# A rotary sum parted between two engines in a fused attention and feed-forward kernel, with all queues laid anew

## The reference, cut to what matters

```python
h = shift_token(x)
q, k, v = jnp.split(h @ wqkv, 3, axis=-1)          # 8 heads of 64
q = l2norm(q) * qs
k = l2norm(k) * ksc
q = q * cos * scale + rotate_half(q) * sin * scale
k = k * cos / scale + rotate_half(k) * sin / scale
o = local_attention(q, k, v)                        # windows of 64
```

## Time and profile before

| what | value |
|---|---|
| time, median of 3 runs | 1863.35 us (1860.35 to 1864.81) |
| the profiled execution's own time | 1865.29 us |
| its span in the trace | 1863.5 us |
| TensorE matmuls busy | 1598.5 us, 86% |
| VectorE busy | 1239.7 us, 67% |
| ScalarE busy | 926.7 us, 50% |
| GpSimd busy | 594.0 us, 32% |

### The profile page before, as it was taken

One profiled execution on the slowest core, in us unless ns is written; L12 is line 12 of the kernel. 1 busy time (PEld: TensorE's weight loads), 2 busy tenths in 40 slices (PEclk: granted clock), 3 DMA queues, 4 the chain that ended last, 5 costly groups with the idle time before them and its releaser, 6 DMA issues.

```text
span 1863.5 us, 29596 instructions
## 1 busy us (share of the span) xinstructions
PE 1598.5 (86%) x11565; PEld 934.8 (50%) x11632; DVE 1239.7 (67%) x2636; ACT 926.7 (50%) x1751; POOL 594.0 (32%) x401
## 2 busy tenths in 40 slices
PE   5688876799979899799988999798996889788978
PEld 2354443446454555546555455545553546445635
DVE  6866767775677657595577756786576447674724
ACT  3465653466543844457544664438443444352241
POOL 2756726151160604324061511606043014110000
PEclk9789998799989999899998999899997899898989
DMA  4200100300131011500123001310114002304102
GB/s 120 66 1 21 27 1 20 69 23 17 41 89 32 22 32 34 111 23 2 41 68 69 22 24 34 92 29 22 32 40 105 3 18 76 78 11 103 37 1 63
DMA packets 37291, 80.12 MB, mean 43 GB/s; under 512 B 6782, under 2 KB 22654, under 8 KB 33776
## 3 DMA queue, kind: packets, MB, share of 16 engines
q1 hardware_dynamic: 37152, 78.22, 16.7%
...
## 4 chain that ended last, share of the span: by engine, by line
PE 47%; DVE 23%; ACT 14%; POOL 12%; issue 4%; DMA 0%; SPq 0%; POOLq 0%; DVEq 0%; ACTq 0%
PE ps L455 42%; POOL fsmall L1348 5%; DVE bsmall L1224 5%; ACT bigs L944 5%; PE ps L460 4%; POOL work L1371 3%; ACT work L870 3%; DVE fsmall L1113 2%; POOL work L1382 2%; POOL bsmall L1348 1%; DVE fsmall L1105 1%; DVE bxn L1021 1%; DVE work L1076 1%; DVE work L1075 1%; DVE fxn L1021 1%
## 5 line engine op out<-in xcount | busy, mean ns | idle before, releaser
L1348 POOL TENSOR_TENSOR fsmall<-fsmall,consts 128x8 f32<-128x8 f32 (+1 forms) x140 | 200.1, 1440 | 330.5 <-DVE fsmall L1015 310.9
L455 PE MATMUL ps<-maskb,identb 128*128 128x128 bf16 (+1 forms) x1122 | 227.8, 239 | 31.3 <-ACT work L870 18.8
L455 PE MATMUL ps<-bxt,mw 128*128 128x512 f32 x504 | 246.7, 610 | 5.9 <-DVE bigs L1320 5.9
L1371 POOL TENSOR_TENSOR work<-work 128x1024 f32<-128x1024 f32 x56 | 132.2, 2360 | 351.0 <-DVE work L1076 351.0
L870 ACT ACTIVATE work<-ps,fsmall 128x128 f32<-128x128 f32 x448 | 164.0, 493 | 71.1 <-DVE fsmall L1117 70.4
L460 PE MATMUL ps<-ident,work 128*128 128x128 f32 x924 | 140.6, 298 | 50.2 <-ACT work L870 42.4
L1224 DVE TENSOR_REDUCE bsmall<-ps 128x1 f32<-128x512 f32 (+3 forms) x308 | 175.3, 631 | 7.5 <-PE ps L455 6.8
L455 PE MATMUL ps<-wqkv,h 128*128 128x512 f32 x336 | 163.4, 618 | 14.1 <-ACT vs L830 8.8
L1402 POOL TENSOR_TENSOR work<-work,fsmall 128x1024 f32<-128x1024 f32 x56 | 106.2, 1897 | 216.1 <-DVE fsmall L1108 216.1
L944 ACT ACTIVATE bigs<-ps 128x512 f32<-128x512 f32 x280 | 146.1, 635 | 24.1 <-PE ps L455 23.7
L966 ACT ACTIVATE bigs<-ps 128x512 f32<-128x512 f32 x126 | 75.3, 598 | 156.6 <-PE ps L455 155.9
...
## 6 DMA issues: line engine op xcount, KB each, us to landing
...
```

Source lines behind the costliest of these rows:

```text
L455: return nc.tensor.matmul(o, a, b, start=start, stop=stop, skip_group_check=True)
L1348: return nc.gpsimd.tensor_tensor(out, x, consts[:, k:k + 1].broadcast_to([x.shape[0], x.shape[1]]), op)
L1371: nc.gpsimd.tensor_tensor(R.qk[:, m, :], R.qk[:, m, :], R.part[m % 2], ALU.add).then_inc(R.l_add.sem, 1)
```

## The change

GpSimd's sum keeps only the keys' half. VectorE sums the queries' half in a new step `qa`, behind both pairs of products, and each half has a signal of its own: `l_add` is now the keys' sum, `l_addq` the queries'. TensorE's transposes of the queries wait for `l_addq`. The reuse of `part` is guarded for each half by its own sum. The orders of four engines and of SyncE's queue are written anew, GpSimd's in its first part alone.

```diff
@@ class Front
-        self.l_rot, self.l_add = sig("l_rotary_products", LAYERS * 4), sig("l_rotary_sum", LAYERS * 4)
+        self.l_rot, self.l_add = sig("l_rotary_products", LAYERS * 4), sig("l_k_rotary_sum", LAYERS * 4)
+        self.l_addq = sig("l_q_rotary_sum", LAYERS * 4)
@@ TensorE, project
-                    pe.wait_ge(R.l_add.sem, R.l_add.at(s, 4 * l + m + 1))
+                    pe.wait_ge(R.l_addq.sem, R.l_addq.at(s, 4 * l + m + 1))
@@ VectorE, rotary
                     if j == 0 and m >= 2:
+                        dve.wait_ge(R.l_addq.sem, R.l_addq.at(s, 4 * l + m - 1))
+                    if j == 1 and m >= 2:
                         dve.wait_ge(R.l_add.sem, R.l_add.at(s, 4 * l + m - 1))
@@ VectorE, project
+                def rotary_sum_q(m):
+                    dve.wait_ge(R.l_rq.sem, R.l_rq.at(s, 4 * l + m + 1))
+                    tt_(R.qk[:, m, 0:INNER], R.qk[:, m, 0:INNER], R.part[m % 2][:, 0:INNER], ALU.add).then_inc(R.l_addq.sem, 1)
...
                     rotary(m, 1)
+                    yield f"qa{m}.{l}"
+                    rotary_sum_q(m)
                     yield f"ss{m}.{l}"
                     square_sums(m)
@@ GpSimd, project
-                    nc.gpsimd.tensor_tensor(R.qk[:, m, :], R.qk[:, m, :], R.part[m % 2], ALU.add).then_inc(R.l_add.sem, 1)
+                    nc.gpsimd.tensor_tensor(R.qk[:, m, INNER:], R.qk[:, m, INNER:], R.part[m % 2][:, INNER:], ALU.add).then_inc(R.l_add.sem, 1)
```

More of the change, by code:

```diff
@@ L56 @@
     "tensor": (
[L57 to L66 removed]
+        "FFBFFFFFBBBFBBFFBFFFFFBFBBFBFFFBBFBFFBFFBFBBFFFFFFBFBFBBBFFBFBBFBFFFBFFFBFBBBFFBFFBFFBBBFFFFBFFFFFBB"
+        "BBBBFBFFBFBBFBFBFFBFFFFFBFBBBBBBBFBBFFFFFFBFBFBFFBFBFFBFFBBBBBBBFBFFFFFBFBFBBBBBFFFBFFFF",
+        "FFBBFFFFFFFFFFFFBBBFBBBFBBBBBBBBBBBBFBFBBFBFBBBFFBBBBFBBBBFBBFBBBFBFBBBBBBFBBBBFBBBBBBBBBBBBBBBBBFBF"
+        "BBBFFBBBBBBBFBFBBBFFBBFBFBBBBBBBBBBFBBBBBBFBBBFBBBFBFBFFFFFBFBBBFBBBBBFBBBBBFBBBBBFFFFFFBFBFBBBBBFBF"
+        "FBFFFFBBBBBBFBFFBFBFFBBBFBBBBFFFBBFFFFFB",
+        "FBBFFFFFFBBBBBBBBBBBBBBBBBBBBFBBBBBBBBBBBBBBBBBBBFBBBBBBBBBBBBBFBFBBBFBBBBBBBFBBBFBBBBFBBBBBBFBBBBBB"
+        "BBBBBBBBBBBBBBBBFFBBBBFBBBBFBFBFFBBBBBFFBBBBBBBBBBBBBBFFBBBBFBBBFBFBBBBBBBFBFFBBFBFFFBFBBBBBBBFBFBBF"
+        "FFFFFFFFFFBBBBFBBBBBBBBBBFBBBBBBBBBBBBFFBBBBBBBBBFBBBBBBFBFBBBFBBFBBBBBBBFBBBBBBBBBBBFBBBBBFBBBBBBBB"
+        "BBBBBBBBBBBBBBBBBBBBBBBBBBBBBBFFFFBFBBFFBBFBFBFFBBBBBBBBBBFFBFBBFFBFFBBFFFBFBBBFBBFFBFFBBFFFBFBBBBFF"
+        "BBFFFBFFFFBFFFBFFBBBFFBFFFFFFFFFBFFFFFFFFFFFFFFFFFFFFFFFFFFFFFFFFFFFFFFFFFFFFFFFFFFFFFFFFFFFFFFFFFFF"
         "FFFFFFFFFFFFFFFFFFFFFFFFFFFFFFFF",
@@ L78 @@
     "vector": (
-        "BFFBFFFFFFFFBFBBBFFFFFBBBFBFFBFFFBBBFFBBFBBFBFBFBFFFFBFFBFFFFBFBBBBBBFBFBBBBFBBFFFBFFFFBFFFFFFFBFBFF"
-        "FFBFFBBBFFBFBFFBBFBBFFFBBFFBBBBBFBFBBBBFBBFFFBFBFFBFBBBFBFBFFFBFFFBFBFFFBFFFFFFFBFBBFBFFBFF",
-        "BFBFFBBBBFFFFFBFFFFFBBFBBBBBBBBBBBFBBBBBBBBBBFFBBFBBBBFBBBBFBBFBBBFBFBBBBBBFBFFFFFFFFFFFFFFFFFFBBFBB"
-        "FFBFBFBBBBBBBFBBFBBBBFFFFBBFBFFBBFBFBFFFFBFFFBFBBFBFFFFBFFFBFFBFFBBFFBBFFB",
-        "BBBBBBFFFFFFFFBFFBBBBBBBBBBBBBBBBBBBBBBBBBBBBBBBBBBBBBBBBBBBBBFBFFFFBBBBFFBFBBBFBBBBBBBFFBBFBBBFFFBB"
-        "BBFBFBBFFFBBBFBFFFFBBFBBBBBFFBBFBFBBBBFFFFFFFBFBBBBBBBBFBBBBBBBBBBBBBFBBBBBBBBBBBBBBBBBBBBBBFBBFFFFB"
-        "FFFFFFBBBBFBBFBFFFBFBBBBBFFFBBFBBFBBBBFFFBFFFFBBFBBFFFFFBBFBFFFBFFFFFBFFFFBBFBFFFFFBFFFBBBFFFFFFFFFF"
-        "FFFFFFFFFFFFFFFFFFFFFFFFFFFBFFF",
+        "BFFBFFFFFFFFBFBBBFFFFFFFFBBBBFFBFFFFBBBBFFFBFBBBBFFBFBBFBFFFBFFBBFFFBBFFBBBFBBFBBBBFBBFBFFBFFFFBFFFF"
+        "FFFFFFBFBFFFFFBFFBBBFFBFFBFBBBFBBFFFBBBFFBBBBBBFBBBFBBBFBFBFFBFBFFBFBBBFBBFFFFBFFFBFBFFFBFFFFFFFFFBF"
+        "FBBFFBFFBFF",
+        "BFBFFBBBBFFFFFFFFFBFBBFBBBBBBBBBBBFBBBBBBBBFBBBBFFBBBBFBBBBFBBFBBBFBFFBBBBBBFFBFFFFFFFFFFFFFFFFFFFFF"
+        "BBBBFFBFBFBBBBBBBFBBFBBBBFBFFFBFBFFBBFBBFFFBFFFFFBFBBBFFFFFFFFBFFFFBBFFFBFFBBFBFFB",
+        "BBBBBBFFFFFFBFFFFBBBBBBBBBBBBBBBBBBBBBBBBBBBBBBBBBBBBBBBBBBBBBFBFFFFBBBBFFBFBBBFBBBBBBBBFFBBFFBBFFFB"
+        "FBBBFFBBFBFFFBBFFBBFFFFBBBBBFBBFFBBFBFBBBBFFFFFFFBFBBBBBBBFBBBBBBBBBBBBBBFBBBBBBBBBBBBBBBBBBFBBBBBBF"
+        "FFBFFFFFFFBBBBBBFBFFFFBFBBBBBFFFBFBFBBBFBFBFFBFFFBFBBFBFBFFFBFBFFFBFFFFBBFBBFFFFBFFFFFFBFFFBBFBFFFFF"
+        "FFFFFFFFFFFFFFFFFFFFFFFFFFFFFBFFFFF",
     ),
     "gpsimd": (
-        "FBFFFFFBFFFFFFBBFFBBFBBFFFFBBBBBBBBBBBFFFFFFFFFFFFFFFBFFBBBBBBBBBBBBBBFBBFFFFFFFFFFFFFF",
+        "FBFFFFFBFFFFFFBBBBFFFBBFFFBFBBBBBBBBBBFFFFFFFFFFFFFFBFFFBBBBBBBBBBBBBBFBBFFFFFFFFFFFFFF",
         "BFFFFFFFFFFFFFFFFFFFFFBFFFFFFFFFFFFFFF",
@@ L93 @@
     "sync": (
-        "BFBFFBFF",
-        "BBFBBFBBBBBBBFB",
-        "BBBBBBBFBBBBBBBBFBBBBBFBFFFFFFFFBFBBF",
+        "FBBFFFBF",
+        "BBBFFBBBBBBBBFB",
+        "BBBBBBBFBBBBBBBBFBBBBBFBBFFFFFFFBFFBF",
     ),
```

22 lines of the change are left out of this document (6 added, 16 removed).

## The result

The changed kernel takes 1876.81 us, the median of 4 runs (1876.31 to 1876.96); the kernel before took 1864.08 on the same chip (4 runs, 1860.35 to 1865.37). The ratio on record is 1.0081, with a 95% interval of 1.006 to 1.0102: slower by 0.8% (the two medians as they stand are 12.7 us apart, 0.7%). The profiled spans are 1874.1 and 1863.5 us, 10.6 apart. The forecast was 1865 in a range of 1850 to 1880, so the range holds the time, and the likeliest value was 12 us too low.

A forecast was written before the change was run, and what follows sets the result against it. VectorE was taken to set the pace, with TensorE and GpSimd nearly full at a turn's end. Terms +2.4, +2.5, +1.5 and -3 gave +3.4 us, shortened to +1.5: forecast 1865 us, range 1850 to 1880.

The forecast's parts named there:

- The chain is no promise; a relieved GpSimd meets VectorE.: At a turn's end: the sum's 3% chain share promises no gain, since VectorE is busy 24.22 of 29 us too.
- Half a sum, 1.18 us, 76 us off GpSimd and 44 on VectorE.: All 64 sums: GpSimd's half takes 1.18 us, saving it 76 us; VectorE's query sums of 0.69 add 44 us.
- The turn's end, +0.4.: Last block's inverse root starts 0.4 us later, held by VectorE's last square sum; six places, +2.4 us.
- GpSimd waits 0.55 us for the port, VectorE comes first.: Shared SBUF port: each query sum starts just before GpSimd's keys' sum, which waits some 0.55 us.
- The second layer, +0.5 for `qa0` and +0.3 for `sm0`.: Beside the maxima, each turn: first query sum exposed, +0.5 us; TensorE's `sm0` one fill later, +0.3 us.
- The five turns: Per turn: +0.4 us at the end, +0.5 and +0.3 in the second layer; other exchanges within full stretches 0.
- The first part, -3: First part, two front halves sharing GpSimd: gains of 6 us less 3 us of exposed query sums, between -9 and +3.
- The last part, 0: Last part: four query sums lie beside the experts, where TensorE is full, so they cost 0.
- The choice to shorten +3.4 to +1.5: Whole kernel: the summed +3.4 us was cut to +1.5, expecting time back from gaps not seen.
- C: Rival, slower: VectorE's queue bounds both stretches, +11.8 us, nothing gained in the first part, 1875 us; chance 0.20.
- B: Rival, faster: GpSimd's relief comes through, 1.2 us gained at each turn's end, 1853 us; chance 0.30.
- D: Rival, slower: GpSimd gets the port first, each query sum stands still 1.18 us, 1888 us; chance 0.10.

The follow-up runs named there:

- e11: Changed kernel with the keys' half of the sum left out on GpSimd, a one-column marker in its place: 1867.55 us, ratio 1.0049.
- e3: Changed kernel with the queries' sum left out on VectorE, a one-column memset in its place: 1855.86 us, ratio 0.9973.
- e4: Changed kernel with each query sum replaced by an equally long VectorE instruction reading one SBUF operand: 1877.34 us, ratio 1.0092.
- e2: The changed kernel's new order without query sums on VectorE, the whole sum on GpSimd as before: 1869.79 us, ratio 1.0054.
- e1: Parted sum as in the change, but the order of the kernel before, each query sum directly behind its keys' products: 1875.87 us, ratio 1.0087.
- e5: Changed kernel with two order exchanges undone in every turn, one on TensorE, one on VectorE: 1879.58 us, ratio 1.0079.
- e12: Changed kernel with two VectorE steps, `var.1` and `qa3.0`, moved in the third sequence's first projection: 1872.49 us, ratio 1.0047.

## Why the forecast was right in its range and wrong in its likeliest value

*The chain is no promise; a relieved GpSimd meets VectorE.* Right. e11 shows it most plainly: with no sum on GpSimd at all, the turn's end keeps its 42.9 us; and e3, where VectorE has no query sums, has 41.6.

*Half a sum, 1.18 us, 76 us off GpSimd and 44 on VectorE.* Too hopeful for GpSimd: 1.27 us undisturbed and 1.65 mostly, outside the 1.15 to 1.25 that I had named as the sign.

*The turn's end, +0.4.* Right, and by the step named: the last root is now released by VectorE's square sum. The measured difference is +0.40, +0.50, +0.41, -0.55 and +0.42 us in the five turns. The odd one, and the 43.4 us that two turns take in the kernel before where three take 42.5, come with TensorE's clock: in the kernel before, the 15.6 us behind `x1` have a granted 0.89 in such a turn (710.9) and 1.00 in one of 42.5 (494.4).

*GpSimd waits 0.55 us for the port, VectorE comes first.* Right for 59 of the 64 query sums, which ran at full pace, with 0.38 us for GpSimd (1.65 for 1.27) and not 0.55; by e4 even these cost the whole nothing. The 1.75 us that I set beside the rule of two inputs belong to a cast, which reads one operand; of the rows of before it is the product on line 1117, two operands and 1.565 us for 0.167, that bears on the form with two inputs. The other five took 0.97 to 2.05 us, three of them in the first part; the longest took 2.05 us at 199.89, until a GpSimd product of 1.90 at 199.49 had ended. VectorE there:

```profile
199.89 2.05 DVE L1093 TENSOR_TENSOR pqs<-pqs,pks 128x512 f32<-128x512 f32 x1
```

And GpSimd:

```profile
199.49 1.90 POOL L1412 TENSOR_TENSOR work<-work,fsmall 128x1024 f32<-128x1024 f32 x1 [2.27 <-DVE fsmall L1118]
```

I had considered only the keys' sum of the same block as GpSimd's rival, not what else GpSimd does in front of it.

*The second layer, +0.5 for `qa0` and +0.3 for `sm0`.* Right in their sum: +0.77, +0.58, +0.78, +0.77 and +0.77. VectorE's timeline after, against the earlier trace rows:

```profile
1049.55 0.69 DVE L1093 TENSOR_TENSOR work<-work 128x512 f32<-128x512 f32 x1
...
1050.76 0.68 DVE L1222 CAST bsmall<-bsmall 32x128 bf16<-32x128 f32 x1
1051.47 1.03 DVE L1224 TENSOR_TENSOR bsmall<-bsmall 32x128 bf16<-32x128 f32 x1
...
1072.76 1.23 DVE L1123 TENSOR_REDUCE fsmall<-ps 128x8 f32<-128x1024 f32 x1 [1.58 <-PE ps L457]
```

The wait for `sm0` is 1.58 us and was 0.88: 0.7 where I had taken half a fill. The cast takes 0.68 us and took 1.75, with `qa1` of 0.60 ahead of it: 1.07 gained for 0.60, which I had called even.

*The five turns.* My terms give 5 x (0.4 + 0.5 + 0.3) = +6.0, and the turns lengthened by 6.1. That is closer than the working deserves: between routing and `x1`, where I priced the exchanges at nothing, each turn loses some 0.4 us (2.1 in five), and clock and gaps elsewhere give 0.8 back. e2 loses the same 0.4 and e1 does not: it is the order's. VectorE waits 1.27 us at 1113.64 in the changed kernel for a TensorE result where it waited 0.17; which of TensorE's exchanges does it was not tried.

*The first part, -3.* This is the step that failed. I wrote "Gains of 1.2 at some five such places, 6 us, less five query sums on the path, 3 us", and had +0.4 for its turn's end. It was +3.2 at the end of the part (325.92); e5, alike up to there, has +0.7, so a part of the miss is one execution's chance. The gain was there, 1.9 us in the changed kernel and 3.9 in e11 between 140 and 160, and was given back before 278.65; then came the 4.2 us, which repeat. What I left out is what the new order and the query sums do between 278.65 and 297.92: VectorE hands TensorE its operand later, TensorE stands and the granted clock falls a second time (1.70 us at six fills). I had read a clock of 1.00 in two stretches of a turn and left it out of the sum for the whole kernel. Standing still beside GpSimd is not shown as the further cost of this place: `var.1` does so in the kernel before too (1.71 us), and what `qa3` loses nothing waits for. It was there to be gained, as e12 shows, and not added by the change.

*The last part, 0.* It was +1.8 up to 1808.56. It is +1.9 in e12 too, but -0.3 in e5, and all three have the same instructions there. So nothing is shown against the 0.

*The choice to shorten +3.4 to +1.5* was wrong in direction. With the terms as they stood the forecast would have been 1867. Of the 9.1 us between +1.5 and the measured +10.6, 5.8 are the first part's, 1.8 the last part's, 0.1 the turns' and 1.9 this choice; 0.5 comes back behind the last mark. Since some 2 us of the first row and all of the last part are within what one execution differs from the next, only the 4.2 us and this choice are safe to name.

*The rivals.* C came nearest (1875, with nothing gained in the first part), and was given 0.20. It was near by luck: it wanted 11 us from the five turns, which gave 6.1, and knew nothing of the 4.2. B is refuted by the turns' ends, which lost 0.4 where it has a gain of 1.2; D's price by the 59 free sums.
